# Reordering TensorE's work behind a gather, packing a transposed operand from four chunks into three, and two idle matmuls in the last tile

## The chip, the cores and the metric

The kernel runs on one core of a Trainium2 chip. The metric is the device time of one execution in microseconds (us). Lower is better. The engines are named as in the profile: PE is TensorE's matmul side, PEld its weight loads, DVE is VectorE, ACT is ScalarE, POOL is GpSimd, SP is SyncE.

## What is computed

A recommendation model's top part: 27 embedding rows of 128 numbers are looked up for each of 512 samples, all pairwise dot products within a sample are taken, 16 dense numbers are appended, and three layers follow.

```python
e = jnp.stack([tbl_0[ids[:, 0]], ..., tbl_26[ids[:, 26]]], axis=1)   # (512, 27, 128), fp32
dot_products = jnp.einsum('bnd,bmd->bnm', e, e)
r, c = np.tril_indices(27, k=-1)
z = dot_products[:, c, r]                                           # (512, 351)
h = jnp.concatenate([z, dense_ctx], axis=1)                         # (512, 367)
h = jnp.maximum(h @ W_top1 + b_top1, 0.0)                           # (512, 512)
h = jnp.maximum(h @ W_top2 + b_top2, 0.0)                           # (512, 256)
y = h @ W_top3                                                      # (512, 1)
```

## The kernel before

The 512 samples are four tiles of 128 (`T = 4`). Every engine has its own hand-written list of calls, and semaphores join the lists. Nothing is reordered by a planner: the order of the calls in the source is the order on the engine.

**The one-hot part.** Nine small tables (1000 rows) are looked up by matmul: DVE and ACT make one-hot matrices, PE multiplies (`one_hot`, L456 and L460), ACT copies the result into `embT` (L224). The other 18 tables are gathered on POOL by one indirect DMA for each table and tile, 72 in all (L214), in tile order. Gathered rows are turned on PE in groups of up to four (`transposes(t, g)`, L470; five groups a tile, the last of two) and copied into `embT` by ACT or DVE (L228). Tile 0's groups and three of tile 1's are worked in between the one-hot matmuls.

**Behind it**, for each tile t:

- `products(t, u)`, u = 0 and 1: 64 small matmuls of 32 x 27 each, one sample each (L487). They are in fp32, and PE runs each as two passes, so the profile counts 128 matmuls and 128 weight loads for a call. ACT copies the result to `prod` (L351), DVE merges the other half of the products over it (L252).
- `turn(t)`: DVE turns 32 x 32 blocks from `prod` to `pairs` in one instruction (L261, 14 columns of 32), then PE transposes `pairs` in four chunks of 112 (L501), and ACT and DVE copy two chunks each to `pairsT` (L356, L266). The 14 columns hold 448 rows, of which 351 are products that the first layer needs and the rest are gaps with zero weights.
- `layer1(t, ms)` (L511): four output blocks of 128, each over the `KC = 4` chunks. `layer2(t)` (L523): 2 output blocks over 4 chunks. `layer3(t)` (L532): one output row over 2 chunks. In between ACT and DVE add the bias and apply ReLU (L365, L275, L373, L283); DVE copies the result row to `y_sb` (L288).

The Gram results use four PSUM banks (`GB = 4`). The transposes of gathered rows use two banks behind the one-hot part, the layers two others, and layer 3's row stands in a corner of one of the latter, which is why `turn(t)` waits for `y_ready` of the tile before. At its start PE runs `WARM = 11` matmuls of 512 columns whose results nobody reads (L538).

Waits that a matmul cannot carry itself are instructions of their own on PE (`pe.wait_ge` twice before one matmul). A fp32 matmul is four PE instructions (two passes, each a load and a matmul), a transpose or a one-hot matmul two.

Of the kernel before, what the change touches and what calls it, by code (L numbers as in the profile page):

```python
# [16 lines left out]
UNIT = 16  # L17
GB = 4
UNITS = GROUPS // UNIT
# [4 lines left out]
MERGED = HALF + 1  # L24
KC = 4
KR = MERGED * SLOT // KC
assert KR * KC == MERGED * SLOT and KR + ND <= P

# [17 lines left out]
MC2 = H2 // P  # L46
WARM = 11


# [16 lines left out]
def tower(nc, ids, ids_t, dense_t, tbls, w1, w2, cols, pick, y):  # L66
# [21 lines left out]
    with ExitStack() as ctx:  # L88
# [22 lines left out]

        pairs = sb("pairs", [P, 2, MERGED * SLOT])

# [15 lines left out]
        layer = [fill[:, 2 + i, :] for i in range(2)]  # L129
        sums3 = layer[1][0:1, 2 * P:3 * P]  # L130

# [22 lines left out]
        prod_a = sem("prod_a")  # L154
        merged = sem("merged")
        pairs_ready = sem("pairs_ready")
        turned = sem("turned")
# [15 lines left out]
        @block.sync  # L173
        def _(sp):
            def load_onehot(n):
                f = ONEHOT[n]
                if n >= NT:

                    sp.wait_ge(filled, FILL_NO[("oh", n - NT)] + 1)
                sp.dma_start(ids_bc[:, n % NT, :], ids_t[f:f + 1, :].broadcast_to([P, B])).then_inc(idsbc_in[n], 16)  # L180
                rows = tbls[f].rearrange("(p c) d -> p (c d)", c=CH)
                sp.dma_start(table[0:CA, n % NT, :], rows[0:CA]).then_inc(table_in[n], 16)
                sp.dma_start(table[CA:CR, n % NT, :], rows[CA:CR]).then_inc(table_in[n], 16)

# [7 lines left out]
            sp.dma_start(pairsT[KR:KR + ND, :, 0, :], dense_t.rearrange("n (t b) -> n t b", t=T)).then_inc(w_in, 16)  # L192
# [39 lines left out]
        def _(dve):  # L232
# [23 lines left out]
            def turn(t):  # L256
                dve.wait_ge(merged, UNITS * (t + 1))
                if t >= 2:

                    dve.wait_ge(turned, t - 1)  # L260
                nc.vector.transpose(pairs[:, t % 2, :].rearrange("p (c i) -> p c i", i=SLOT),  # L261
                                    prod[:, t % 2, :, :].rearrange("p g c -> p c g")).then_inc(pairs_ready, 1)

            def take_turned(t):
                dve.wait_ge(turned, t + 1)
                nc.vector.tensor_copy(pairsT[0:KR, t, 2:4, :],  # L266
                                      layer[1][0:KR, 0:2 * P].rearrange("p (k b) -> p k b", k=2)).then_inc(pairsT_v, 1)

# [34 lines left out]
            take_turned(0)  # L303
            take_products(1, 0)
            take_layer1(0)
            take_transposes((2, 0))
            take_layer2(0)
            take_products(1, 1)
            turn(1)
            take_layer3(0)  # L310
            take_transposes((2, 1))
            take_turned(1)
            take_transposes((2, 2))
            take_layer1(1)
            take_transposes((2, 3))
            take_layer2(1)
            take_transposes((2, 4))
            take_layer3(1)
            take_products(2, 0)
            take_transposes((3, 0))  # L320
            take_products(2, 1)
            turn(2)
            take_transposes((3, 1))
            take_turned(2)
            take_transposes((3, 2))
            take_layer1(2)
            take_layer2(2)
            take_layer3(2)
            take_transposes((3, 3), (3, 4))
            for u in range(UNITS):  # L330
# [8 lines left out]
        def _(act):  # L339
# [14 lines left out]
            def take_turned(t):  # L354
                act.wait_ge(turned, t + 1)
                nc.scalar.copy(pairsT[0:KR, t, 0:2, :],  # L356
                               layer[0][0:KR, 0:2 * P].rearrange("p (k b) -> p k b", k=2)).then_inc(pairsT_a, 1)

# [46 lines left out]
            act.wait_ge(zeros_ready, 1)  # L405
            take_products(0, 0)
            take_transposes((1, 3))
            take_products(0, 1)
            take_transposes((1, 4))
            take_turned(0)  # L410
            take_products(1, 0)
            take_layer1(0)
            take_transposes((2, 0))
            take_layer2(0)
            take_products(1, 1)
            take_transposes((2, 1))
            take_turned(1)
            take_transposes((2, 2))
            take_layer1(1)
            take_transposes((2, 3))  # L420
            take_layer2(1)
            take_transposes((2, 4))
            take_products(2, 0)
            take_transposes((3, 0))
            take_products(2, 1)
            take_transposes((3, 1))
            take_turned(2)
            take_transposes((3, 2))
            take_layer1(2)
            take_layer2(2)  # L430
            take_transposes((3, 3), (3, 4))
            for u in range(UNITS):
# [6 lines left out]
        def _(pe):  # L439
# [51 lines left out]
            def turn(t):  # L491
                pe.wait_ge(pairs_ready, t + 1)
                if t == 0:

                    pe.wait_ge(taken_a, len(EARLY))
                else:

                    pe.wait_ge(h2_a, t)
                    pe.wait_ge(y_ready, t)
                for k in range(KC):  # L500
                    last = nc.tensor.transpose(layer[k // 2][0:KR, k % 2 * P:(k % 2 + 1) * P],  # L501
                                               pairs[:, t % 2, k * KR:(k + 1) * KR], ident[:])
                last.then_inc(turned, 1)

            def layer1(t, ms):
                pe.wait_ge(pairsT_a, t + 1)
                pe.wait_ge(pairsT_v, t + 1)
                for m in ms:
                    for k in range(KC):
                        rows = KR + ND if k == 0 else KR  # L510
# [16 lines left out]
            def layer3(t):  # L527

                pe.wait_ge(h2_v, t + 1)
                pe.wait_ge(h2_a, t + 1)  # L530
                for m2 in range(MC2):
# [5 lines left out]
            for _ in range(WARM):  # L537
                nc.tensor.matmul(fill[:, 3, :].rearrange("p (r c) -> p r c", r=4), ident[:],  # L538
                                 ident[:].unsqueeze(1).broadcast_to([P, 4, P]), start=True, stop=True)
            for what in EARLY:  # L540
# [4 lines left out]
            pe.wait_ge(zeros_ready, 1)  # L545
            products(0, 0)
            transposes(1, 3)
            products(0, 1)
# [10 lines left out]
            transposes(2, 1)  # L559
            turn(1)  # L560
            transposes(2, 2)
            layer1(1, (0, 1))
            layer1(1, (2, 3))
            transposes(2, 3)
            layer2(1)
            transposes(2, 4)
            layer3(1)
            products(2, 0)
            transposes(3, 0)
            products(2, 1)  # L570
            transposes(3, 1)
            turn(2)
            transposes(3, 2)
            layer1(2, (0, 1))
            layer1(2, (2, 3))
            layer2(2)
            layer3(2)
            transposes(3, 3)
# [50 lines left out]
```

## Time and profile before

| | |
|---|---|
| median of 3 runs | 178.98 us (178.2 to 181.49) |
| the profiled execution | 177.67 us |
| its span, first to last instruction | 175.8 us |
| outside the span | 1.87 us |
| mean granted TensorE clock | 0.806 of full |
| busy: PE, PEld, DVE, ACT, POOL | 104.6, 82.8, 55.5, 48.3, 78.8 us |

All durations below are of the one profiled execution. The span has three stages: the one-hot part (0 to 52 us), a stretch in which POOL goes on gathering and PE is mostly idle (52 to 110 us), and the rest of tiles 0 to 3 on PE (110 to 176 us). "Issue" as the cause of an idle time means that the engine waited for nothing that the profile shows.

### The profile page before, as it was taken

Reading aid. Unit: us, or ns where it says so; the run is one execution under the profiler, and the core shown is the slowest. Engines: PE = TensorE matmul, PEld = TensorE weight load, DVE = VectorE, ACT = ScalarE, POOL = GpSimd, SP = SyncE. Lnnn points to the kernel's source line nnn. Section 1 sums busy time; section 2 is a strip of 40 time slices with the busy share of each in tenths; the row PEclk is TensorE's granted clock in tenths of the full one; section 3 lists DMA queues with packets and bytes.
Section 4 is the critical chain, followed back from the end, with each engine's and each line's share of the span. In section 5 each row is a group of like instructions: output and inputs, shape, how many; then the busy total and the mean of one; then the engine's idle time right before and its main releaser. Section 6 shows DMA issues by size and latency. Waiting matters only on the chain.

```text
span 175.8 us, 3411 instructions
## 1 busy us (share of the span) xinstructions
PE 104.6 (59%) x1486; PEld 82.8 (47%) x1486; DVE 55.5 (32%) x112; ACT 48.3 (27%) x84; POOL 78.8 (45%) x79
## 2 busy tenths in 40 slices
PE   6999999599982111100000002958969547972794
PEld 2448887487862110000000001748869437951693
DVE  5586978989700000000000000150343134123111
ACT  0581985999931000000000000311322111220010
POOL 4778877878777777777777730000000000000000
PEclk9999999999999555555555555599999996999579
DMA  4999999995121212121212110000000000000000
GB/s 76 278 256 267 346 273 247 240 241 122 34 60 49 60 45 60 45 60 45 60 45 60 51 38 0 4 4 4 4 0 0 4 4 4 0 4 4 0 4 0
DMA packets 6571, 13.59 MB, mean 77 GB/s; under 512 B 2422, under 2 KB 2998, under 8 KB 6428
## 3 DMA queue, kind: packets, MB, share of 16 engines
q1 hardware_dynamic: 4252, 8.64, 19.4%
q0 software_dynamic: 2304, 4.72, 9.9%
q8 instruction: 12, 0.20, 0.4%
q14 instruction: 3, 0.02, 0.0%
HBM read 13.36 MB, written 0.00 MB: 76 GB/s over the span
## 4 chain that ended last, share of the span: by engine, by line
issue 39%; PE 31%; POOL 21%; DVE 4%; DMA 3%; ACT 1%
POOL emb L214 21%; PE fill L511 10%; PE gram L487 10%; PE fill L523 4%; PE fill L470 3%; PE fill L501 2%; DVE pairs L261 2%; DMA emb<-tbl_dram,ids_sb 1%; DMA ids_sb<-ids_dram 1%; PE fill L532 1%; DVE prod L252 1%; DVE h L283 1%; ACT prod L351 1%; DVE pairsT L266 0%; ACT embT L228 0%
## 5 line engine op out<-in xcount | busy, mean ns | idle before, releaser
L214 POOL DMA_INDIRECT emb<-tbl_dram,ids_sb x72 | 78.0, 1084 | 23.2 <-issue 21.6
L487 PE MATMUL gram<-embT 128*32 128x27 f32 x1024 | 18.5, 202 | 56.0 <-issue 55.5
L487 PEld LDWEIGHTS gram<-embT 128*32 128x32 f32 x1024 | 14.9, 117 | 60.1 <-issue 59.1
L252 DVE COPY_PREDICATED prod<-pick_sb,gram 128x224 f32<-128x224 int32 x8 | 3.3, 407 | 79.7 <-ACT prod L351 79.7
L238 DVE TENSOR_SCALAR onehot<-ids_bc,row_no 125x512 fp32r<-125x512 int32 x63 | 26.0, 482 | 6.2 <-DMA ids_bc<-ids_t_dram 3.9
L351 ACT COPY prod<-gram 128x224 f32<-128x224 f32 x8 | 2.8, 345 | 72.6 <-PE gram L487 72.6
L511 PE MATMUL fill<-pairsT,w_sb 112*128 112x128 f32 (+1 forms) x128 | 18.3, 309 | 2.4 <-issue 1.6
L456 PE MATMUL fill<-onehot,high 125*128 125x512 f32 x72 | 19.2, 408 | 0.0
L511 PEld LDWEIGHTS fill<-pairsT,w_sb 112*128 112x128 f32 (+1 forms) x128 | 17.5, 222 | 3.3 <-issue 1.8
L460 PE MATMUL fill<-onehot,low 125*128 125x512 f32 x72 | 17.9, 390 | 0.0
L460 PEld LDWEIGHTS fill<-onehot,low 125*128 125x128 f32 x72 | 13.5, 188 | 2.9
L456 PEld LDWEIGHTS fill<-onehot,high 125*128 125x128 f32 x72 | 13.0, 188 | 3.2 <-issue 0.5
L470 PE MATMUL fill<-ident,emb 128*128 128x128 f32 x72 | 12.6, 299 | 2.5 <-DMA emb<-tbl_dram,ids_sb 2.4
L538 PE MATMUL fill<-ident 128*128 128x512 f32 x22 | 11.6, 692 | 1.6 <-POOL ident L204 1.6
L224 ACT COPY embT<-fill 128x512 f32<-128x512 f32 x9 | 10.0, 1112 | 7.8 <-PE fill L460 7.5
L241 DVE TENSOR_TENSOR low<-table,high 125x1024 fp32r<-125x1024 f32 x9 | 10.9, 1216 | 1.3 <-ACT high L391 1.3
L470 PEld LDWEIGHTS fill<-ident,emb 128*128 128x128 f32 x72 | 9.0, 151 | 4.9 <-issue 4.1
L391 ACT CAST high<-table 125x512 fp32r<-125x512 f32 x18 | 10.4, 628 | 2.7 <-DMA table<-tbl_dram 2.5
L228 ACT COPY embT<-fill 128x512 f32<-128x512 f32 (+1 forms) x14 | 9.4, 670 | 5.6 <-PE fill L470 5.5
L538 PEld LDWEIGHTS fill<-ident 128*128 128x128 f32 x22 | 4.9, 228 | 7.5 <-issue 5.9
L523 PE MATMUL fill<-h,w_sb 128*128 128x128 f32 x64 | 8.4, 279 | 0.0
L275 DVE TENSOR_SCALAR h<-fill,cols_sb 128x128 f32<-128x128 f32 x8 | 2.4, 347 | 18.5 <-PE fill L511 18.5
(25 smaller groups left out, 51.1 us busy)
## 6 DMA issues: line engine op xcount, KB each, us to landing
table<-tbl_dram SPq DMA_DIRECT2D x9, 448.0 KB
ids_bc<-ids_t_dram SPq DMA_DIRECT2D x9, 256.0 KB, 5.0
emb<-tbl_dram,ids_sb POOLq DMA_INDIRECT x72
w_sb<-w_dram SPq DMA_DIRECT2D x1, 1024.0 KB
w_sb<-w_dram SPq DMA_DIRECT2D x1, 512.0 KB
table<-tbl_dram SPq DMA_DIRECT2D x9, 52.0 KB
ids_sb<-ids_dram SPq DMA_DIRECT2D x1, 54.0 KB, 2.1
pairsT<-dense_t_dram SPq DMA_DIRECT2D x1, 32.0 KB
```

The costliest lines, as they stand in the source:

```text
L214: nc.gpsimd.indirect_dma_start(out=emb[:, t % EB, n, :], out_offset=None, in_=tbls[f], in_offset=bass.IndirectOffsetOnAxis(ap=ids_sb[:, t, ...
L224: copy(embT[:, :, :, what[1]].rearrange("p t b -> p (t b)"), fill[:, bank(i), :]).then_inc(taken, 1)
L238: nc.vector.tensor_scalar(onehot[:, n % 2, c, :], ids_bc[0:CR, n % NT, :], row_no[0:CR, c:c + 1], None, ALU.is_equal).then_inc(onehot_v, 1)
L241: nc.vector.tensor_tensor(low[:, n % 2, :], table[:, n % NT, :], high[:, n % 2, :].bitcast(fp32), ALU.subtract).then_inc(low_ready, 1)
L391: nc.scalar.copy(high[:, n % 2, a:a + half], table[:, n % NT, a:a + half]).then_inc(high_ready, 1)
L456: nc.tensor.matmul(fill[:, bank(i), :], high[:, n % 2, c * D:(c + 1) * D], onehot[:, n % 2, c, :], start=(c == 0), stop=False)
L460: last = nc.tensor.matmul(fill[:, bank(i), :], low[:, n % 2, c * D:(c + 1) * D], onehot[:, n % 2, c, :], start=False, stop=(c == CH - 1))
L470: last = nc.tensor.transpose(fill[:, bank(i), (n - a) * P:(n - a + 1) * P], emb[:, t % EB, n, :], ident[:])
L487: last = nc.tensor.matmul(gram[i % GB][SLOT * s:SLOT * (s + 1), g, :], embT[:, t, b, :], embT[:, t, b, 0:F], start=True, stop=True)
L511: last = nc.tensor.matmul(layer[m // 2][:, m % 2 * P:(m % 2 + 1) * P], w1_sb[0:rows, k, m * P:(m + 1) * P], pairsT[0:rows, t, k, :], start ...
L523: last = nc.tensor.matmul(layer[m2][:, 0:P], w2_sb[:, m, m2 * P:(m2 + 1) * P], h1[:, m, :], start=(m == 0), stop=(m == MC - 1))
L538: nc.tensor.matmul(fill[:, 3, :].rearrange("p (r c) -> p r c", r=4), ident[:], ident[:].unsqueeze(1).broadcast_to([P, 4, P]), start=True, ...
```

## The change

Four things are changed.

1. **Three chunks.** `prod`'s 13 full columns are turned so that the rows follow each other without gaps (row 13*i + c), and the half column is laid behind them by a second DVE instruction, which waits for the first. 364 rows and the 16 dense ones fit three chunks (128, 128, 108), so `turn` has three PE transposes, `layer1` twelve matmuls rather than sixteen for a tile, DVE copies one chunk rather than two, and `w1` is 768 KB rather than 1024 KB. The host lays the weights out to match.
2. **The order.** On PE both halves of `products` stand together for every tile. In tile 0 they run ahead of the last transposes of tile 1; in tile 1 both halves run ahead of layer 1 of tile 0; `turn(1)` moves ahead of layer 3 of tile 0; further transposes of the next tile are spread between the layers. DVE's and ACT's lists are changed to match.
3. **PSUM.** Layer 3's row gets a bank of its own, `GB` goes from 4 to 3. `turn(t)` waits for `h2_v` of the tile before in place of `y_ready`, and `layer3` waits for `y_ready`.
4. **Idle matmuls.** Two matmuls of 512 columns whose result is not read (`TURN_BUSY = 2`, four passes) stand between `products(3, 1)` and `turn(3)`.

```diff
-GB = 4
+GB = 3
-KC = 4
-KR = MERGED * SLOT // KC
+TURNED = HALF * SLOT
+ROWS = HALF * F + HALF
+KC = 3
+KL = ROWS - (KC - 1) * P
+TURN_BUSY = 2
...
-        sums3 = layer[1][0:1, 2 * P:3 * P]
+        sums3 = pb("sums3", [1, P])[:]
...
-                nc.vector.transpose(pairs[:, t % 2, :].rearrange("p (c i) -> p c i", i=SLOT),
-                                    prod[:, t % 2, :, :].rearrange("p g c -> p c g")).then_inc(pairs_ready, 1)
+                by_column = prod[:, t % 2, :, :].rearrange("p g c -> p c g")
+                nc.vector.transpose(pairs[:, t % 2, :].rearrange("p (i c) -> p c i", c=HALF),
+                                    by_column[:, 0:HALF, :]).then_inc(columns_ready, 1)
+                dve.wait_ge(columns_ready, t + 1)
+                nc.vector.transpose(pairs[:, t % 2, HALF * F:HALF * F + SLOT],
+                                    by_column[:, HALF, :]).then_inc(pairs_ready, 1)
...
                     pe.wait_ge(h2_a, t)
-                    pe.wait_ge(y_ready, t)
+                    pe.wait_ge(h2_v, t)
                 for k in range(KC):
-                    last = nc.tensor.transpose(layer[k // 2][0:KR, k % 2 * P:(k % 2 + 1) * P],
-                                               pairs[:, t % 2, k * KR:(k + 1) * KR], ident[:])
+                    rows = KL if k == KC - 1 else P
+                    last = nc.tensor.transpose(layer[k // 2][0:rows, k % 2 * P:(k % 2 + 1) * P],
+                                               pairs[:, t % 2, k * P:k * P + rows], ident[:])
...
+            def keep_busy(b, count):
+                for _ in range(count):
+                    nc.tensor.matmul(fill[:, b, :].rearrange("p (r c) -> p r c", r=4), ident[:],
+                                     ident[:].unsqueeze(1).broadcast_to([P, 4, P]), start=True, stop=True)
...
-            products(1, 0)
+            for u in range(UNITS):
+                products(1, u)
             layer1(0, (0, 1))
             layer1(0, (2, 3))
             transposes(2, 0)
             layer2(0)
-            products(1, 1)
+            turn(1)
...
                 products(3, u)
+            keep_busy(0, TURN_BUSY)
             turn(3)
```

The order on PE, from the last one-hot matmul to tile 2's products. `gram0` to `gram3` are the products' banks, `fill<-ident,emb` are transposes of gathered rows, `fill<-ident,pairs` those of `turn`, and the last three kinds are layers 1, 2 and 3. The kernel before:

```order
L487 MATMUL gram0<-embT 32x27 x64
L470 MATMUL fill<-ident,emb 128x128 x4
L487 MATMUL gram1<-embT 32x27 x64
L470 MATMUL fill<-ident,emb 128x128 x2
L501 MATMUL fill<-ident,pairs 112x128 x4
L487 MATMUL gram2<-embT 32x27 x64
L511 MATMUL fill<-pairsT,w1_sb 128x128 x16
L470 MATMUL fill<-ident,emb 128x128 x4
L523 MATMUL fill<-h1,w2_sb 128x128 x8
L487 MATMUL gram3<-embT 32x27 x64
L532 MATMUL fill<-h2,cols_sb 1x128 x2
L470 MATMUL fill<-ident,emb 128x128 x4
```

The changed kernel, the same stretch on PE:

```order
L494 MATMUL gram0<-embT 32x27 x64
L494 MATMUL gram1<-embT 32x27 x64
L477 MATMUL fill<-ident,emb 128x128 x6
L509 MATMUL fill<-ident,pairs 128x128 x2
L509 MATMUL fill<-ident,pairs 108x128
L494 MATMUL gram2<-embT 32x27 x64
L494 MATMUL gram0<-embT 32x27 x64
L519 MATMUL fill<-pairsT,w1_sb 128x128 x12
L477 MATMUL fill<-ident,emb 128x128 x4
L531 MATMUL fill<-h1,w2_sb 128x128 x8
L509 MATMUL fill<-ident,pairs 128x128 x2
L509 MATMUL fill<-ident,pairs 108x128
```

Tile 1's second half of products moved from behind layer 2 of tile 0 to ahead of its layer 1, the turn of tile 1 now directly follows layer 2 of tile 0, and layer 1 has 12 matmuls.

The order on PE for the end of tile 2 and all of tile 3, the kernel before:

```order
L487 MATMUL gram<-embT 32x27 x64
L470 MATMUL fill<-ident,emb 128x128 x4
L487 MATMUL gram<-embT 32x27 x64
L470 MATMUL fill<-ident,emb 128x128 x4
L501 MATMUL fill<-ident,pairs 112x128 x4
L470 MATMUL fill<-ident,emb 128x128 x4
L511 MATMUL fill<-pairsT,w_sb 128x128 x16
L523 MATMUL fill<-h,w_sb 128x128 x8
L532 MATMUL fill<-h,cols_sb 1x128 x2
L470 MATMUL fill<-ident,emb 128x128 x6
L487 MATMUL gram<-embT 32x27 x128
L501 MATMUL fill<-ident,pairs 112x128 x4
```

The changed kernel, the same stretch:

```order
L494 MATMUL gram<-embT 32x27 x128
L477 MATMUL fill<-ident,emb 128x128 x8
L509 MATMUL fill<-ident,pairs 128x128 x2
L509 MATMUL fill<-ident,pairs 108x128
L477 MATMUL fill<-ident,emb 128x128 x4
L519 MATMUL fill<-pairsT,w_sb 128x128 x12
L477 MATMUL fill<-ident,emb 128x128 x4
L531 MATMUL fill<-h,w_sb 128x128 x8
L543 MATMUL sums<-h,cols_sb 1x128 x2
L477 MATMUL fill<-ident,emb 128x128 x2
L494 MATMUL gram<-embT 32x27 x128
L549 MATMUL fill<-ident 128x512 x2
```

The transposes between the two halves of tile 2's products moved behind both, four of the next ones moved between layers 1 and 2, and the two idle matmuls stand behind tile 3's products.

## Rows read from the trace of the kernel before

**Rows 1.** Three stages: us, busy us of each engine (instructions), granted clock, DMA share, GB/s

```profile
0.00:52.00 52.00, 48.00 (x192) 34.23 (x192) 38.27 (x74) 34.86 (x53) 40.19 (x39) 1.00 0.80 205
52.00:110.00 58.00, 8.20 (x100) 5.54 (x104) 0.00 (x0) 1.27 (x2) 38.62 (x41) 0.54 0.17 48
110.00:176.00 66.00, 48.38 (x1202) 43.02 (x1201) 17.22 (x38) 12.15 (x30) 0.00 (x0) 0.89 0.01 3
```

**Rows 2.** Timeline, end of the slow stretch: start, us, instruction, count, idle before

```profile
101.87 0.94 POOL L214 DMA_INDIRECT emb<-tbl_dram,ids_sb  x1 [0.30 <-issue]
...
103.58 0.20 PE L487 MATMUL gram<-embT 128*32 128x27 f32 x1 [2.60 <-issue]
...
109.88 0.79 PE L487 MATMUL gram<-embT 128*32 128x27 f32 x40 [1.15 <-issue]
```

**Rows 3.** The chain that ended last, 110 to 162 us: start, us, what

```profile
110.66 1.05 PE fill L470 x4
111.71 1.86 PE gram L487 x128
...
116.12 1.22 PE gram L487 x82
...
117.75 1.60 issue
...
128.61 0.63 PE fill L501 x4
...
129.84 3.81 PE fill L511 x32
133.65 0.44 PE fill L470 x4
134.09 1.80 PE fill L523 x16
...
137.99 1.97 issue
...
141.95 1.84 issue
...
158.23 1.93 issue
```

**Rows 4.** PE's timeline between two stops, 139 to 144 us

```profile
139.96 0.25 PE L487 MATMUL gram<-embT 128*32 128x27 f32 x3 [1.97 <-issue]
140.14 0.66 PE L470 MATMUL fill<-ident,emb 128*128 128x128 f32 x4
140.72 1.22 PE L487 MATMUL gram<-embT 128*32 128x27 f32 x120
```

**Rows 5.** DMA queue that carries instructions: packets, MB, share of 16 engines' span

```profile
q8 instruction: 12, 0.20, 0.4%
```

**Rows 6.** The chain that ended last, tiles 2 and 3

```profile
145.92 1.10 PE fill L501 x4
...
161.11 0.35 ACT prod L351
...
161.93 0.95 DVE pairs L261
...
162.93 1.11 PE fill L501 x4
164.06 0.43 DVE pairsT L266
...
164.63 6.05 PE fill L511 x32
...
173.21 0.61 PE fill L532 x4
```

**Rows 7.** A stretch at the lower clock: columns as in rows 1

```profile
162.50:169.30 6.80, 5.76 (x26) 5.38 (x27) 0.80 (x2) 1.00 (x3) 0.00 (x0) 0.50 0.01 2
```

**Rows 8.** The first idle matmuls (L538) alone: PE, PEld, clock, DMA share, GB/s

```profile
5.50:9.00 3.50, 3.50 (x9) 1.56 (x9) 1.00 1.03 266
```

More of the change, by code:

```diff
@@ L24 @@
 MERGED = HALF + 1
-KC = 4
-KR = MERGED * SLOT // KC
-assert KR * KC == MERGED * SLOT and KR + ND <= P
+TURNED = HALF * SLOT
+ROWS = HALF * F + HALF
+KC = 3
+KL = ROWS - (KC - 1) * P
+assert 0 < KL and KL + ND <= P
 ROWS_OH = 1000
@@ L110, in tower @@
         prod = sb("prod", [P, 2, GROUPS, MERGED])
-        pairs = sb("pairs", [P, 2, MERGED * SLOT])
+        pairs = sb("pairs", [P, 2, TURNED])
         pairsT = sb("pairsT", [P, T, KC, P])
@@ L307, in _ @@
             take_layer2(0)
-            take_products(1, 1)
-            turn(1)
+            take_turned(1)
+            take_transposes((2, 1))
             take_layer3(0)
-            take_transposes((2, 1))
-            take_turned(1)
+            take_layer1(1)
             take_transposes((2, 2))
-            take_layer1(1)
+            take_layer2(1)
             take_transposes((2, 3))
-            take_layer2(1)
+            take_layer3(1)
             take_transposes((2, 4))
[L318 to L321, printed above, removed]
+            for u in range(UNITS):
+                take_products(2, u)
             turn(2)
-            take_transposes((3, 1))
+            take_transposes((3, 0), (3, 1))
             take_turned(2)
@@ L355, in take_turned @@
                 act.wait_ge(turned, t + 1)
-                nc.scalar.copy(pairsT[0:KR, t, 0:2, :],
-                               layer[0][0:KR, 0:2 * P].rearrange("p (k b) -> p k b", k=2)).then_inc(pairsT_a, 1)
+                nc.scalar.copy(pairsT[:, t, 0:2, :],
+                               layer[0][:, 0:2 * P].rearrange("p (k b) -> p k b", k=2)).then_inc(pairsT_a, 1)
             def take_layer1(t):
@@ L405, in _ @@
             act.wait_ge(zeros_ready, 1)
[L406 to L409, printed above, removed]
+            for u in range(UNITS):
+                take_products(0, u)
+            take_transposes((1, 3), (1, 4))
             take_turned(0)
-            take_products(1, 0)
+            for u in range(UNITS):
+                take_products(1, u)
             take_layer1(0)
@@ L414, in _ @@
             take_layer2(0)
-            take_products(1, 1)
+            take_turned(1)
             take_transposes((2, 1))
-            take_turned(1)
+            take_layer1(1)
             take_transposes((2, 2))
-            take_layer1(1)
-            take_transposes((2, 3))
             take_layer2(1)
[L422 to L426, printed above, removed]
+            take_transposes((2, 3), (2, 4))
+            for u in range(UNITS):
+                take_products(2, u)
+            take_transposes((3, 0), (3, 1))
             take_turned(2)
@@ L530, in layer3 @@
                 pe.wait_ge(h2_a, t + 1)
+                if t > 0:
+                    pe.wait_ge(y_ready, t)
                 for m2 in range(MC2):
@@ L534, in layer3 @@
                 last.then_inc(layer3_ready, 1)
+            def keep_busy(b, count):
+                for _ in range(count):
+                    nc.tensor.matmul(fill[:, b, :].rearrange("p (r c) -> p r c", r=4), ident[:],
+                                     ident[:].unsqueeze(1).broadcast_to([P, 4, P]), start=True, stop=True)
             pe.wait_ge(ident_ready, 1)
-            for _ in range(WARM):
-                nc.tensor.matmul(fill[:, 3, :].rearrange("p (r c) -> p r c", r=4), ident[:],
-                                 ident[:].unsqueeze(1).broadcast_to([P, 4, P]), start=True, stop=True)
+            keep_busy(3, WARM)
             for what in EARLY:
@@ L545, in _ @@
             pe.wait_ge(zeros_ready, 1)
-            products(0, 0)
+            for u in range(UNITS):
+                products(0, u)
             transposes(1, 3)
-            products(0, 1)
             transposes(1, 4)
@@ L551, in _ @@
             turn(0)
-            products(1, 0)
+            for u in range(UNITS):
+                products(1, u)
             layer1(0, (0, 1))
@@ L556, in _ @@
             layer2(0)
-            products(1, 1)
+            turn(1)
+            transposes(2, 1)
             layer3(0)
-            transposes(2, 1)
-            turn(1)
-            transposes(2, 2)
             layer1(1, (0, 1))
             layer1(1, (2, 3))
+            transposes(2, 2)
+            layer2(1)
             transposes(2, 3)
-            layer2(1)
+            layer3(1)
             transposes(2, 4)
-            layer3(1)
-            products(2, 0)
+            for u in range(UNITS):
+                products(2, u)
             transposes(3, 0)
-            products(2, 1)
             transposes(3, 1)
@@ L575, in _ @@
             layer1(2, (2, 3))
+            transposes(3, 3)
             layer2(2)
             layer3(2)
-            transposes(3, 3)
             transposes(3, 4)
@@ L608 @@
             hi, lo = max(ORDER[i], ORDER[j]), min(ORDER[i], ORDER[j])
-            row = SLOT * c + i
-            w1[row % KR, row // KR] = w_top1[hi * (hi - 1) // 2 + lo]
+            w1[HALF * F + i if c == HALF else HALF * i + c] = w_top1[hi * (hi - 1) // 2 + lo]
             pick[:, i, c] = j >= HALF
-    w1[KR:KR + ND, 0] = w_top1[F * (F - 1) // 2:]
+    w1[ROWS:ROWS + ND] = w_top1[F * (F - 1) // 2:]
+    w1 = w1.reshape(KC, P, H1).transpose(1, 0, 2)
     ids = give("ids_dram", inputs["ids"])
```

18 lines of the change are left out of this document (10 added, 8 removed).

## The prediction, made before the changed kernel was run

> **What bounds the kernel now.** I read three views in this order: the busy time by stage, the chain that ended last, and PE's timeline where that chain says "issue".
>
> By stage [rows 1], the first 52 us are the one-hot part, in which PE is busy 48.0 us. The change leaves it alone but for a weight load 256 KB smaller. From 52 to 110 us PE is busy 8.2 of 58 us, DVE 0, and POOL gathers. From 110 to 176 us POOL is done, and PE is busy 48.4 of 66 us. All that the change touches is in this third stage, and only what stands on its chain counts.
>
> The second stage is strange. PE stands in `products(0, 0)`, which waits for nothing, yet its matmuls come 2.80 us apart (idle 2.60) until shortly after POOL's last gather at 101.87 [rows 2]. At 109.88 it suddenly runs 40 in 0.79 us. I can't name the cause. But PE's program up to the end of `products(0, 0)` is the same in both kernels, instruction for instruction, and so are the gathers. I take that stretch as unchanged, and count from 110.66, where the first of tile 1's transposes starts [rows 3].
>
> In the third stage the chain is nearly all PE, with four idle pieces put down to "issue": 1.60, 1.97, 1.84 and 1.93 us, 7.34 in all [rows 3]. Between the one that ends at 139.96 and the next, which begins at 141.95, PE ran 3 + 4 + 120 = 127 passes [rows 4]. Each is a load and a matmul, so 254 instructions, and two separate waits make 256. The queue that carries instructions moved 12 packets, 0.20 MB [rows 5], which is 16 KB each. So PE's program comes in **blocks of 256 instructions**, and these four pieces are PE waiting for a block. From the start of `products(1, 0)` at 116.12, four instructions ahead of a block's end, to the end of the stop at 117.75 + 1.60 = 119.35 it is 3.24 us. From 139.96 to 141.95 + 1.84 = 143.79 it is 3.83. I read this as a new block being there 3.2 to 3.8 us after the one before it is entered. Work with long passes covers that: 32 passes of layer 1 take 3.81 us [rows 3]. Products don't: 128 passes, a whole block, take some 1.3 us (1.22 for 120 [rows 4]), which leaves about 2 us idle.
>
> The Trainium skill, "Runtime: NRT & Kernel Launch", section "Instruction fetch mechanics", also has 16 KiB blocks of 256 instructions, but says that the cost of crossing from one to the next is "mostly hidden". Here it isn't. By that rule the later stops of the walk below would vanish and the result would be about 8 us lower.
>
> **The change part by part**, as a walk from 110.66. The places of the blocks' ends in the new program follow from counting on from the stops of before.
>
> *Tile 0.* The second half of the products follows at once: 110.66 + 1.86 at the lower clock [rows 3] = 112.5. From the end of products to the start of the turn on PE it is 162.93 - 161.11 = 1.82 us (ACT copy, DVE merge, DVE transpose) [rows 6]. The DVE transpose is now two instructions with a wait between them. No row shows the short one, or an output written with a stride of 13. Less than nothing is excluded, since the elements are almost the same and an instruction is added. At the other end I set a second full transpose, 0.95 us [rows 6]. I take 0.2, near the low end, as 416 + 32 columns are the 448 of before. So `turn(0)` is at 114.6. The six transposes of tile 1 fit ahead of it (110.66 to 111.71 for four at the lower clock). Three chunks take 0.47 in place of 0.63, and `products(1, 0)` starts at 115.1 in place of 116.12: **1.0 us won**.
>
> *Tile 1's products in one piece.* They cross two block ends, one 7 instructions in, one 6 instructions into layer 1. First stop: ends at 115.1 + 3.24 = 118.35. Second: 1.24 us of products, then layer 1 stops until 118.35 + 3.2 to 3.8, and I take 122.0. Before, layer 1 ran on from 119.35. So this place **loses 2.6 us**, a new stop of some 2.3 us, though the second half of the products, 1.3 us, is now behind us.
>
> *Layers of tile 0.* Layer 1 has 24 passes rather than 32. At 3.81/32 = 0.119 each [rows 3] that is 2.86 us, **0.95 less for each tile**. Then transposes 0.44 and layer 2 1.80: end at 126.85. The bias step (about ACT's 0.35, and 0.1 of signalling) is now open, since the products that covered it are gone: `turn(1)` at 127.3. Before it was 128.61, because ACT, DVE merge and transpose stood behind the second half of the products. **1.3 us ahead.**
>
> *Tile 1.* Turn 0.47, transposes 0.44, layer 3 about 0.5 (0.61 [rows 6] at most), and layer 1 starts at 128.7 (before 129.84). The copies to `pairsT` are under the transposes. Then 2.86 + 0.44 + 1.80 = 133.8 (before 135.89). Behind it transposes 0.44, layer 3 0.5, two transposes 0.3 and their copy some 0.5: tile 2's products start at 135.7. **1.0 us ahead** of 136.7 (137.99 less 125 passes).
>
> *Tile 2's products in one piece.* Block ends fall 30 instructions into either half. The first stop ends 3.3 after the start, as before (136.7 to 139.96): 139.0. The other 113 passes end at 140.15. The next block end is now behind them, in `transposes(3, 2)`, and due only at 142.8. Before, a second stop of 1.84 stood ahead of the products' end at 144.1. Turn at 140.15 + 1.82 + 0.2 = 142.2, with eight transposes of 0.88 beneath, against 145.92 [rows 6]: **3.7 ahead**. Layer 1 at 143.3, layer 1, transposes, layer 2: 148.5. Layer 3, two transposes and copies some 1.9: products of tile 3 at 150.4. Before it was 156.5 (158.23 less 173 passes). **6.1 ahead.**
>
> *Tile 3.* The block end falls 401 instructions into the products. Stop until 150.4 + 3.75 = 154.15 (before 156.5 to 160.16, 3.7), the last passes 0.6: end at 154.8, **6.3 ahead**. ACT's and DVE's chain of 1.82 + 0.2 makes the turn due at 156.8. Beneath it are the four passes of 512 columns. Nine took 3.50 us at full clock [rows 8], 0.39 each, so 1.6 us, and they end at 156.4: hidden by 0.4 us. Then the clock: before, it fell at 162.5 behind the stop of 1.93 and the idle wait for the turn, and stayed at 0.50 until 169.3 [rows 7]. The last turn took 1.10 in place of 0.63, layer 1 6.05 in place of 3.81 [rows 3, 6]. If the idle matmuls keep it up, the turn takes 0.47, the copies 0.43 and some 0.15, and layer 1 starts at 157.85 (164.63 before, 6.8 ahead), takes 2.86 and not 6.05: **10.0 ahead**. The rest is as before.
>
> *Nothing:* `GB = 3`, since by then each bank was merged long ago, hidden by the stops above (without them a wait of some 0.4). `layer3`'s wait for `y_ready`: DVE copies the row long ahead. DVE and ACT get their calls in the order in which PE delivers; at 17.2 and 12.2 us busy of 66 [rows 1] they queue for at most one copy. The smaller `w1` is covered by the gathers.
>
> **Sum.** 1.0 - 2.6 + 2.9 (to `turn(1)`) - 0.3 (to tile 2's products) + 2.7 (tile 2's stop and turn) + 2.4 (its layers) + 0.2 + 0.5 (to the last layer 1) + 3.2 (that layer 1) = 10.0. The span becomes 165.8, the profiled execution 177.67 - 10.0 = 167.7. The median of the runs is 1.3 above that execution, so the forecast is 178.98 - 10.0 = **169.0**.
>
> **Rivals.**
>
> *The clock falls all the same.* Two stops of 2 us in tile 1 lie nearer to each other than those before which the clock fell at 162.5, and in tile 3 the four passes leave the stop itself idle. In tile 3: 24 passes at 6.05/32 = 0.189 rather than 0.119 cost 1.7, the turn 0.35, and the idle matmuls at half speed take 3.2, 1.2 past the turn's due time: 3.2, so **172.2**. In tile 1 as well, 1.7 more: 173.9. Against it: the stop of 1.60 at 117.75 left the clock up, and the idle matmuls fill most of the second gap.
>
> *Stops at their longer price, and a dear transpose.* Three stops 0.6 longer, and 0.75 more for the DVE transpose at three tiles where it is open: 4.0, so **173.0**.
>
> *The slow stretch lasts longer (the slower side).* If the stretch ends by a place in the program or by what the queue behind holds, not by the gathers' end, then the 64 products that now follow directly may be caught in it. One pass costs 2.80 there [rows 2]. The new order wins back 10.0, so from four more slow passes on the change loses; ten give 178.98 - 10 + 28 = **197**. For it: nobody knows why the stretch ends. Against it: the program is identical until then, and 40 of `products(0, 0)`'s own passes already ran fast.
>
> *The order does nothing.* If the chain's gains in tiles 1 and 2 are eaten by waits that I don't see (`turn(1)` and `layer3` have new ones) and the clock falls, the shorter layer 1 is left: 3.8 less, so **175.2 to 177**.
>
> **How the numbers follow.** Forecast 0.55 (167 to 171.5), clock 0.2, longer stops 0.1, order does nothing 0.08, slow stretch 0.05, and 0.02 for a result far below. The range is 166.5 (all stops at 3.2) to 174.5 (clock falling in both places). No change within 2% (175.4 to 182.6) is about what a measurement of this kernel can't tell from none. Faster 0.86, same 0.08, slower 0.06.
>
> **What would show it.** Right: an idle piece of some 2 us inside tile 1's products and another at the head of layer 1, one inside tile 2's and one inside tile 3's, and the granted clock at 1.00 through the last layer 1, with its 24 passes near 2.9 us. Wrong: a slow stretch that ends later than 110 us, DVE transposes well over 1.1 us together, the idle matmuls ending behind `pairs`, or a last layer 1 of 4.5 us.

## The result, and the profile after

The changed kernel takes 172.63 us (median of 4 runs, 171.64 to 174.67), the kernel before beside it 179.5 (178.2 to 181.49). The ratio is 0.962, with a 95% interval of 0.950 to 0.974: **faster**. The profiled execution took 171.64 us, its span is 169.8. The forecast was 169.0, the range 166.5 to 174.5. Medians in this document are over all runs of a kernel, ratios and their intervals over its fast runs alone (those within 1.5% of its fastest).

The three stages of the profile after, in the columns of [rows 1] (the cuts are where its stages end), and two short stretches of tile 3:

```profile
0.00:52.00 52.00, 48.47 (x192) 34.45 (x192) 38.16 (x74) 34.66 (x53) 40.68 (x37) 1.00 0.78 199
52.00:111.40 59.40, 8.44 (x89) 5.61 (x89) 0.00 (x0) 1.52 (x2) 39.71 (x42) 0.52 0.16 48
111.40:169.80 58.40, 43.12 (x1173) 36.69 (x1173) 17.62 (x42) 12.18 (x30) 0.00 (x0) 0.93 0.01 3
156.90:160.30 3.40, 3.40 (x59) 1.99 (x59) 1.56 (x3) 0.35 (x1) 0.00 (x0) 0.50 0.02 5
161.80:164.80 3.00, 3.00 (x27) 3.00 (x28) 0.03 (x1) 0.63 (x2) 0.00 (x0) 1.00 0.00 0
```

The third stage is 58.4 us long. Before, it was 175.8 - 109.88 = 65.9. So it gave 7.5 us, and the stage ahead of it took 1.55 back: the slow stretch, in which PE's passes come up to 2.80 us apart, ended at 111.43 and not at 109.88. POOL's last gather began 1.5 later too, at 103.40 and not at 101.87 [rows 2]. The last two lines show the clock low during the idle matmuls and full in the last layer 1.

The chain that ended last, after (start, us, what), where [rows 3, 6] show it before:

```profile
116.66 1.32 PE gram L494 x85
117.98 2.45 issue
120.43 1.26 PE gram L494 x81
121.69 0.53 PE fill L519 x3
122.22 1.78 issue
124.00 2.61 PE fill L519 x21
...
129.37 0.52 PE fill L509 x3
...
137.87 1.39 PE gram L494 x87
139.26 1.93 issue
...
152.62 1.90 PE gram L494 x117
154.52 2.35 issue
156.87 0.96 PE gram L494 x41
157.84 3.16 PE fill L549 x4
161.00 0.34 PE fill L509 x3
...
161.80 2.93 PE fill L519 x24
```

There are two stops in tile 1, one of them three passes into layer 1, one in tile 2, one in tile 3. Then come the idle matmuls (L549): four passes in 3.16 us. Layer 1 takes 2.93 where [rows 6] has 6.05.

### The profile page after: what moved, and what is told of

It is laid out like the page before. It is cut to its first block, busy times and chain, and to the rows that moved or that the text cites. A ratio compares the mean times of both kernels' runs of the same rounds, so it can differ in the third digit from the quotient of the medians.

```text
span 169.8 us, 3351 instructions
## 1 busy us (share of the span) xinstructions
PE 100.0 (59%) x1454; PEld 76.8 (45%) x1454; DVE 55.8 (33%) x116; ACT 48.4 (28%) x84; POOL 80.4 (47%) x79
## 4 chain that ended last, share of the span: by engine, by line
issue 41%; PE 29%; POOL 23%; DMA 3%; DVE 2%; ACT 0%
POOL emb L219 23%; PE gram L494 11%; PE fill L519 7%; PE fill L531 4%; PE fill L477 3%; PE fill L549 2%; DMA emb<-tbl_dram,ids_sb 1%; PE sums L543 1%; DMA ids_sb<-ids_dram 1%; PE fill L509 1%; DVE h L292 1%; DVE pairs L267 1%; DVE embT L233 0%; DVE prod L257 0%; ACT pairsT L365 0%
## 5 line engine op out<-in xcount | busy, mean ns | idle before, releaser
L219 POOL DMA_INDIRECT emb<-tbl_dram,ids_sb x72 | 79.6, 1106 | 23.1 <-issue 21.6
L549 PE MATMUL fill<-ident 128*128 128x512 f32 x26 | 15.4, 757 | 1.6 <-POOL ident L209 1.6
L477 PE MATMUL fill<-ident,emb 128*128 128x128 f32 x72 | 11.8, 290 | 3.5 <-DMA emb<-tbl_dram,ids_sb 3.5
L519 PE MATMUL fill<-pairsT,w_sb 128*128 128x128 f32 (+1 forms) x96 | 11.9, 279 | 2.3 <-issue 1.8
L519 PEld LDWEIGHTS fill<-pairsT,w_sb 128*128 128x128 f32 (+1 forms) x96 | 11.1, 191 | 2.9 <-issue 2.2
L549 PEld LDWEIGHTS fill<-ident 128*128 128x128 f32 x26 | 6.2, 248 | 9.1 <-issue 7.4
L531 PEld LDWEIGHTS fill<-h,w_sb 128*128 128x128 f32 x64 | 7.6, 192 | 0.2 <-DVE h L284 0.2
```

The lines of the kernel that those rows point to most:

```text
L219: nc.gpsimd.indirect_dma_start(out=emb[:, t % EB, n, :], out_offset=None, in_=tbls[f], in_offset=bass.IndirectOffsetOnAxis(ap=ids_sb[:, t, ...
L477: last = nc.tensor.transpose(fill[:, bank(i), (n - a) * P:(n - a + 1) * P], emb[:, t % EB, n, :], ident[:])
L531: last = nc.tensor.matmul(layer[m2][:, 0:P], w2_sb[:, m, m2 * P:(m2 + 1) * P], h1[:, m, :], start=(m == 0), stop=(m == MC - 1))
L549: nc.tensor.matmul(fill[:, b, :].rearrange("p (r c) -> p r c", r=4), ident[:], ident[:].unsqueeze(1).broadcast_to([P, 4, P]), start=True, ...
```

## The experiments

Single runs of one kernel spread by 2 to 8.5 us here. The profiles show one source: the slow stretch ends with POOL's gathers, whose last one began anywhere from 101.9 to 106.8 us. I therefore also give the **tail**, the time from PE's return to its full pace (the first of a long row of passes without gaps) to the end of the span: 65.9 us before, 58.4 after. A tail still holds what the granted clock did. It was at 0.50 when the pace came back and rose only later, at 115.9 us in the changed kernel's profile.

### The parts of the change, one at a time

These four ran beside each other on one chip, and the slow stretch was there in all of them. First the changed kernel again.

> The changed kernel once more, as the yardstick for the three beside it. Expected 172.6 us (0.96 of before), with four stops of 1.8 to 2.5 us behind the start of tile 1's products.

Measured: 173.03 us median, ratio 0.949 (0.938 to 0.961). Tail 171.8 - 112.97 = 58.8. There are four stops, but not of the expected length:

```profile
118.58 1.95 PE gram L494 x131
120.53 1.21 issue
121.73 1.92 PE gram L494 x125
...
124.59 0.99 issue
...
140.85 2.20 issue
...
156.39 2.35 issue
```

The granted clock was 0.50 until 124.9 us here, and tile 1's products took 1.9 us for a block rather than 1.3. The two stops shrank from 2.45 and 1.78 to 1.21 and 0.99. From the start of the products to the end of the first stop it is 3.15 us, from there to the end of the second 3.85, at the lower clock as at the full one (3.77 and 3.57). So PE waits for something that comes at its own pace, and a stop is what the passes leave of it. That is also why the tail is only 0.4 us longer, though the clock was low for 7.4 us more of it (11.9 rather than 4.5 us).

Without the idle matmuls:

```diff
-TURN_BUSY = 2
+TURN_BUSY = 0
```

> The changed kernel without the two idle matmuls ahead of the last turn. Theory: in the profiled execution they ran at the lower clock, took 3.2 us and ended 1.0 us past the turn's due time, but the clock was back up for layer 1. Without them the turn comes 1.0 earlier and the clock stays low through it and layer 1, as before the change: 24 passes at 0.189 rather than 0.122 us cost 1.6, the turn 0.4. Net 1.0 us slower, 173.6. Rival (the clock comes back by itself, the matmuls only delay): 1.0 us faster, 171.6. Second rival (they were what brought most of the gain): 176 or more.

Measured: ratio 0.956 (0.940 to 0.971). Its six runs lie between 171.6 and 178.4 us, the median of all is 177.37. Tail 175.7 - 113.34 = 62.4. The end of its chain, and the clock there:

```profile
160.63 1.00 PE gram L494 x41
...
163.71 0.92 PE fill L509 x3
...
165.09 5.48 PE fill L519 x24
```

```profile
160.30:170.60 10.30, 7.38 (x85) 6.86 (x85) 1.84 (x4) 1.34 (x4) 0.00 (x0) 0.50 0.01 2
122.80:129.60 6.80, 5.29 (x58) 4.94 (x46) 1.55 (x3) 0.97 (x3) 0.00 (x0) 0.50 0.02 5
```

From the end of the products (161.6) the turn comes after 2.1 us rather than 3.1, and then layer 1 takes 5.48 rather than 2.93 and the turn 0.92 rather than 0.5. Net 2.0 us in tile 3, as by the first theory and twice its price. The other 1.6 of the tail goes with the clock falling at 122.8, ahead of anything that the idle matmuls could touch: layer 1 of tile 0, behind its stop, took 4.46 us and not 2.61. The runs alone don't settle the price. The median is 4.3 us above that of `again`, which would be the second rival (176 or more), but two of the six runs (171.6 and 173.6) are as fast as the changed kernel's, and the intervals of the ratios overlap. The profiles show the 2.0 for tile 3, in one execution of each. What the idle matmuls do to the clock is firmer: the last layer 1 took 2.93 us in all ten profiles that have them and three chunks, and 5.48 and 5.03 in the two that have three chunks and no idle matmuls (here and in the next kernel).

The three chunks alone:

```diff
-TURN_BUSY = 2
+TURN_BUSY = 0
...
-            keep_busy(0, TURN_BUSY)
...
(PE's, DVE's and ACT's calls behind the one-hot part in the order of before)
```

> The three chunks alone, with the calls in the order of before, three banks for the products and layer 3's row in a bank of its own, no idle matmuls. Theory: 8 of 32 passes of layer 1 go for each tile: 0.95 in tiles 0 and 1, about 1.1 in tile 2, 1.5 in tile 3 at the lower clock, the turn 0.2 shorter each time, the second DVE transpose 0.24 longer on the chain of three tiles: 4.5 us less than before, so 175.0 us (ratio 0.975). Rival (the packing is hidden under the stops for instruction blocks): less than 2 us less, 177.5 or more.

Measured: 174.73 us median, ratio 0.968 (0.960 to 0.975). Tail 173.8 - 114.90 = **58.9**, that is 7.0 less than before and only 0.1 to 0.5 more than the whole change. By the medians the whole change is 1.7 us ahead of it. The two profiled executions also differ by 1.9 in where the slow stretch ended, so the runs can't tell how much of the 1.7 is of the kernel. Its idle pieces put down to "issue", behind 115 us:

```profile
119.27 1.55 issue
124.18 0.58 issue
142.10 1.37 issue
157.14 2.35 issue
```

The first lies ahead of tile 0's turn, as does 1.31 before, and ends as DVE's transposes of `pairs` end (120.72), so it isn't counted as a stop. The other three make 4.3 us, where [rows 3] has 7.34. The sixteen passes that shorter layers take out of two tiles moved the block ends, and tile 2 has one stop in place of two. That is 3.0 us. Layer 1 gives the rest: 5.03 for 6.05 in the last tile, 2.9 for 4.15 and 3.81 in tiles 2 and 1, about 0.8 in tile 0, 4.0 in all. A part of that is the clock, which fell once more in the profile before (145.4 to 148.9).

The new order alone, with the idle matmuls, on four chunks:

```diff
-KC = 3
...
+KC = 4
+KR = MERGED * SLOT // KC
...
(one DVE transpose, 448 rows with gaps, two chunks for DVE to copy, as before)
```

> The new order with the idle matmuls, three banks and layer 3's own bank, but four chunks with gaps as before. Theory: the changed kernel plus 8 passes of layer 1 in each of four tiles (0.12 each, 3.8 us in all) plus 0.5 for the turns, less 0.7 for the second DVE transpose: 172.6 + 3.6 = 176.2 us (ratio 0.98). Rival (the order is worth nothing, the packing all): the time of before, 179.5. Rival (the order is all): 173.

Measured: 180.33 us median beside 181.97, ratio 0.998 (0.987 to 1.009). Tail 177.9 - 114.15 = 63.8, 2.1 less than before. Its stops:

```profile
120.60 2.11 issue
124.39 1.89 issue
...
143.40 2.37 issue
147.52 1.98 issue
...
163.06 1.94 issue
```

That is 10.3 us of stops, 3 more than before, with two in each of tiles 1 and 2. What the idle matmuls win (layer 1 of tile 3 takes 3.81 us here, 6.05 before) the extra stops take back, and 2.1 us of the tail is left. The runs show no gain that is clear of noise. I had expected 176.2: the sum of parts failed, because the block ends fall elsewhere when the program is longer.

### What the slow stretch hangs on

Six profiles so far put PE's return to its full pace 7.9 to 8.15 us behind the start of the last gather. Three kernels were to tell why.

```diff
             pe.wait_ge(zeros_ready, 1)
+            a, e = TG[NTG - 1]
+            pe.wait_ge(gathered[T - 1][NTG - 1], 16 * (e - a))
             for u in range(UNITS):
                 products(0, u)
```

> The changed kernel, with one more wait on PE: it starts the products of tile 0 only when the last gathered rows of tile 3 have landed. So far the slow stretch ended 7.9 to 8.1 us after the start of POOL's last gather, in six profiled executions in which that gather started anywhere from 101.9 to 106.8 us. Theory 1 (PE's instructions come slowly only while gathers are under way, and a landing is some 3 us after the start): PE starts 3 us after the last gather's start, runs both halves of the products in 3.7 us at the lower clock and one stop for a block of 2 us: 2 to 4 us faster than the changed kernel, 169 us. Theory 2 (PE has a fixed number of slow instructions to get through, some 100 at 0.7 us or more each, whenever it comes to them): 50 us or more slower, 225 us. Theory 3 (the slow state ends 8 us after the last gather, whatever PE does): no change, 172 us.

The same with tile 2's last rows, `gathered[T - 2]`:

> The same wait, but for the last gathered rows of tile 2, some 25 us earlier (PE starts the products near 83 us). Theory 1 expects the first 30 to 40 passes fast, then a slow stretch from 83 us until 8 us after the last gather, and no change in time, 172. Theory 2 expects the slow stretch to last 55 us from 83 on, 197. A third possibility is that no slow stretch appears at all: then products of tile 0 end at 86 us, and the time falls to some 165.

And without the gathers of tile 3:

```diff
-            for t in range(T):
+            for t in range(T - 1):
...
-                pe.wait_ge(gathered[t][g], 16 * (e - a))
+                pe.wait_ge(gathered[t % EB][g], 16 * (e - a))
```

> The changed kernel without tile 3's 18 gathers (54 rather than 72); tile 3 is computed on tile 0's gathered rows, so its results are not the reference's. Theory 1: the slow stretch ends 18 x 1.25 = 22.5 us earlier, near 89 us, and the whole takes some 150 us. Theory 2 (a fixed number of slow instructions): the slow stretch still ends near 110 us, 172 us.

They landed on another chip, and there the **kernel before itself takes 131.78 us** (12 runs, 130.6 to 134.9), 48 less. Measured: `hold` 171.8 (six runs), `hold_mid` 148.1 and `no_tile3` 123.4 (one run each). No slow stretch is seen in any of the three profiles. Here is `hold` on that chip, PE's timeline:

```profile
108.76 2.13 PE L494 MATMUL gram<-embT 128*32 128x27 f32 x142 [51.71 <-issue]
112.75 1.80 PE L494 MATMUL gram<-embT 128*32 128x27 f32 x114 [1.86 <-issue]
```

So the three say nothing of what the stretch hangs on. They showed that it isn't a property of the kernel alone. `hold` was therefore run again and came to a third chip, where the kernel before takes 182.56 us.

> The changed kernel with PE held until the last gathered rows of tile 3 have landed. On a chip without the slow stretch it takes 171.8, some 43 us more than the kernel that isn't held. On a chip with the slow stretch it tells what the stretch hangs on. Theory 1 (PE is slow only while gathers are under way): PE starts full speed at the last gather's start + 3 us: 2 to 4 us less than the changed kernel. Theory 2 (a fixed number of slow instructions): 50 us or more added. Theory 3 (PE's slow state lasts until 8 us after the last gather whatever it does): no change.

Measured: 174.9 us, beside 172.0 for the changed kernel. PE's timeline:

```profile
108.55 0.75 PE L494 MATMUL gram<-embT 128*32 128x27 f32 x40 [51.65 <-issue]
109.96 0.20 PE L494 MATMUL gram<-embT 128*32 128x27 f32 x1 [0.65 <-issue]
...
113.46 0.20 PE L494 MATMUL gram<-embT 128*32 128x27 f32 x1 [0.50 <-issue]
114.16 3.10 PE L494 MATMUL gram<-embT 128*32 128x27 f32 x212 [0.50 <-issue]
```

The gathers had landed, PE ran 40 passes, and then it was slow all the same, until 114.16. The last gather began at 105.95, 8.2 us ahead. Theory 1 falls, since no gather was under way, and so does theory 2, since far fewer than 100 instructions were slow. Theory 3 stands: the state ends some 8 us behind the start of the last gather, whether PE is held or not. Holding PE back wins nothing.

This profile also answers a question of the forecast. Its clock fell at 124.8, in tile 1, and stayed at 1.00 through tile 3. There the idle matmuls ran as foretold:

```profile
163.34 1.98 PE L549 MATMUL fill<-ident 128*128 128x512 f32 x4
165.51 0.55 PE L509 MATMUL fill<-ident,pairs 128*128 128x128 f32 x3 [0.20 <-DVE pairs L271]
```

At the full clock the four passes take 1.98 us and end 0.2 ahead of `pairs`, in `hold_mid` and `shift` too. At the lower one they take 3.1 to 3.5 and end behind it.

### Is the new order worth anything?

```diff
 (the three chunks alone, as above, and)
+            keep_busy(0, TURN_BUSY)
             turn(3)
```

> The three chunks and the idle matmuls, but the calls in the order of before. It separates the new order from the rest. From the profiles, from the end of the slow stretch to the end of the span it is 65.9 us before, 58.4 and 58.8 changed, 58.9 with the three chunks alone. Theory: the idle matmuls win 2.0 here as in the comparison of the changed kernel with and without them, so 57 us and a ratio to before near 0.945 to 0.955, as good as the changed kernel or 1.5 us better, and the new order is worth nothing. Rival: the order is worth 2 to 3 us, and this kernel stays 2 us behind the changed one.

On the chip without the slow stretch: 127.96 us, ratio 0.958 (0.950 to 0.967). The stages there, columns as in [rows 1]:

```profile
0.00:52.00 52.00, 47.90 (x188) 34.04 (x189) 38.11 (x74) 34.64 (x52) 40.71 (x37) 1.00 0.82 197
52.00:110.00 58.00, 41.07 (x1072) 35.63 (x1072) 13.90 (x33) 11.73 (x26) 40.34 (x43) 0.85 0.21 52
```

PE is busy 41 of the 58 us in which it is busy 8.2 in [rows 1], and what it waits for most is the gathered rows:

```profile
PE fill L479 <- DMA emb<-tbl_dram,ids_sb: 14.3, 8, 4.0
```

Then, beside the changed kernel on the third chip:

> The changed kernel again, beside the two below on whatever chip they get. The last four kernels ran on another chip than those ahead of them, and there the kernel before takes 131.8 us and no slow stretch is seen in the kernels that don't hold PE back. If this chip has the slow stretch: 173 us, ratio 0.955. If not: PE is free from 56 us on and waits for gathered rows instead. Then both halves of tile 1's products wait for nothing that comes late (tile 1 has landed by 64 us), tile 2's wait for its last rows, landed near 83 us, and tile 3's for the last, landed near 108; only tile 3's own work stands behind those: transposes, products with a stop, the turn, its layers. There the change saves 8 passes of layer 1 and keeps the clock: 3 to 5 us less than 131.8, so 128, ratio 0.97.

> The three chunks and the idle matmuls in the order of before, beside the changed kernel. On a chip without the slow stretch it took 128.0 (ratio 0.958). With the slow stretch: 171 to 172 if the new order is worth nothing, and 174 or more if the order is worth 2 us or more.

Measured: 171.96 and 172.96 us, the first at a ratio of 0.947 (0.936 to 0.957), tails 58.7 and 59.9. The second's layer 1 of tile 0 ran at the lower clock in the profiled execution (4.13 us for 21 passes, 2.61 in the first), which is more than the whole difference. By the medians the new order, with the three chunks and the idle matmuls in place, is worth 1 us at most. By the fastest runs (169.94 and 169.57) it is worth nothing.

### Do the stops follow the blocks?

```diff
+SHIFT = 14
...
             keep_busy(3, WARM)
+            for _ in range(SHIFT):
+                nc.tensor.matmul(fill[0:1, 3, 0:1], ident[:, 0:1], ident[:, 0:1], start=True, stop=True)
```

> The changed kernel with 14 matmuls of one column behind the first idle ones, results not read: 56 more instructions on PE ahead of everything else, which moves every block's end 56 instructions earlier in the program, and costs well under 1 us itself. Theory of the blocks: the next block is asked for some 50 instructions behind a block's start. In the changed kernel that point stood 43 instructions inside tile 1's products, now it stands ahead of them, so the block behind is there in time: tile 1's products and the head of layer 1 show one stop of 2 us rather than two with 3.8 to 4.5 together; tiles 2 and 3 keep one stop each, tile 3's some 0.3 longer. From the end of the slow stretch to the end of the span 56.8 us rather than 58.7: 171 us on a chip that has the slow stretch. And the slow stretch itself: so far some 40 passes ran fast ahead of it, which is where the point 50 instructions behind a block's start lies (the products start 30 behind that start). If the slow state hangs on that point, only 10 to 14 passes run fast now. If it hangs on a count from the products' start, it stays 40. Rival to both: the stops come from the products' own length, wherever the blocks end; then two stops remain in tile 1, the tail stays at 58.7, and the time is that of the changed kernel.

This one came to a fourth chip, again without the slow stretch (before 132.11 us), so nothing is learned of the stretch. Measured: 126.06 us, ratio 0.963 (0.946 to 0.981). PE's timeline:

```profile
68.11 1.61 PE L495 MATMUL gram<-embT 128*32 128x27 f32 x103
71.50 2.09 PE L495 MATMUL gram<-embT 128*32 128x27 f32 x128 [1.78 <-issue]
75.23 0.54 PE L495 MATMUL gram<-embT 128*32 128x27 f32 x25 [1.64 <-issue]
75.70 4.48 PE L520 MATMUL fill<-pairsT,w_sb 128*128 128x128 f32 x24
...
110.87 1.67 PE L495 MATMUL gram<-embT 128*32 128x27 f32 x172 [0.56 <-issue]
114.62 0.91 PE L495 MATMUL gram<-embT 128*32 128x27 f32 x84 [2.08 <-issue]
```

Tile 1's stop moved from pass 131 to pass 103, tile 3's from 200 to 172: 28 passes, 56 instructions, to the pass. Between two stops there are 128 passes. So the rival falls, and the stops do hang on the blocks of 256. But my count of stops was wrong. Tile 1 still has two (1.78 and 1.64, 3.4 in all, where the changed kernel has 4.2 in its first profile). In tile 2 the second block end slipped back into the products (stops of 2.48 and 1.50 us). For tile 1 my guess is that the point at which the next block is asked for stands on the wait that heads the products, not ahead of it; no run tests that. The order, a shift and a packing each only move these places.

## Why the prediction was right, and by its own steps

**Span and blocks.** The reading that "PE's program comes in blocks of 256 instructions" held to the pass, in the changed kernel as in the shifted one. That the stops are waits for a block has a second sign in the trace before: around the stop that begins at 137.99, one packet of 16 KB went over the instruction queue (stretch 137.0 to 139.9):

```profile
q8 instruction: 1, 0.02, 2.1%
```

Behind 110 us that queue moved ten packets in the kernel before, and there were four stops. The other six left no stop. The changed kernel's four stops stood at the places of the walk. Together they were 8.5 us (2.45, 1.78, 1.93, 2.35); by the walk, some 8.

**Step by step.** The walk's times against the profile: `products(1, 0)` 115.1 and 116.6, layer 1 of tile 0 resumed 122.0 and 124.0, `turn(1)` 127.3 and 129.4, tile 2's products 135.7 and 137.9, `turn(2)` 142.2 and 144.5, tile 3's products 150.4 and 152.6, the last layer 1 157.85 and 161.8, end 165.8 and 169.8. So it is 4.0 late, of which 1.55 is the start. The forecast gain of 10.0 us came to 6.0 in the profiled spans and 6.9 in the medians.

**"I take that stretch as unchanged."** Right for the program, too bold for the time. The stretch ends with POOL's last gather, which moves by 5 us between executions; here it was 1.5 later. That is not of the change.

**"Hidden by 0.4 us"** was the term that failed. The idle matmuls ran at the lower clock, which fell at 156.9 behind the stop of 2.35, and took 3.16 rather than 1.6: 1.0 us lost. Even at the full clock four passes take 1.98 (`hold_b`), so the margin was 0.2. This is half of the rival "the clock falls all the same". The other half did not come: at 160.3 it was full again, and layer 1 took 2.93 (2.86 foretold).

**Stops.** The first in tile 1 ended 0.6 later than foretold, the one in tile 3 0.5, with 0.3 for the passes behind it: small steps towards the rival of longer stops. The two DVE transposes took 0.93 + 0.23 against 0.95 and added 0.2 to the chain, as taken.

**"The order does nothing"** was priced at 175.2 to 177 and given 0.08, for the time. The time is not there, but the claim about the order is nearly true. I gave tile 2's single stop (2.7 us) to the order. The three chunks alone get it too, because they shorten the program. So the total was right and its shares were wrong, and that the total held is in part luck: packing 7.0 of the tail, idle matmuls 1.1 to 2.0 in tile 3 where layer 1 would else run slowly, order at most 1. (The 1.1 is the same stretch, from the end of the products to the end of layer 1, in `pack_only` and `pack_idle_b`: 8.5 and 7.35 us.) The three don't add up to the whole, since each moves the block ends for the others.

**The rule of the Trainium skill** ("Runtime: NRT & Kernel Launch", "Instruction fetch mechanics") that a crossing is "mostly hidden" does not hold for these rows of 128x27 matmuls. All profiled kernels show stops there, most of 1.1 to 2.7 us, the shortest 0.5. Six of the ten blocks behind 110 us in the kernel before do cross without a stop. Its block size agrees.

**Left open:** what the slow stretch is. It was there in the first comparison and on two chips since, in every kernel profiled, and on two other chips in none (the kernel before was not profiled there, only timed). Each chip was used in one comparison only, so nothing here tells the chip from the moment. It costs some 50 us of 180. Its end follows the last gather's start by 7.9 to 8.4 us in nine profiles, held or not. That PE should wait on something left by POOL's gathers is argued from this, not shown. Another sign points at the supply of instructions: in all nine profiles a packet on the instruction queue starts within 0.7 us of the end of the first quick passes, at 53.8 and 53.2 us before, at 109.6 and 109.3 in `hold_b`. So the slow stretch may set in where the next block is asked for. `shift` was to test that and came to a chip without the stretch. It wasn't tried to fill the stretch with other work or to spread the gathers over time. Whether the whole change gains as much on a chip without the stretch wasn't measured either: only two relatives of it ran there, at 0.958 and 0.963.

## What to carry to other kernels

Short matmuls in a long row outrun the supply of instructions: here 128 passes take 1.3 us, and the next 256 instructions were there 3.1 to 4.1 us after a block was entered. Count instructions on PE as a cost of their own, and prefer an edit that removes them to one that reorders them; before crediting a new order with a stop that went, count where the blocks' ends fall. And when one execution differs from the next, look for the stage: a tail measured from a common event tells 1 to 2 us apart where the runs spread by 8, if the falls of the clock within it are looked up first.

## What the hardware showed that I had not expected

The same kernel took 131.8 and 132.1 us on two chips and 179.5 to 182.6 on the others. The difference is about as long as the stretch in which PE issues a pass, at first every 0.7 to 2.8 us and from 90 us on every 2.80, with nothing to wait for. It sets in after some 40 passes, even when PE starts only after all the gathers have landed.

The granted clock does not fall in the same place in every execution. Kernels alike up to there had the same stop of 2.35 us inside tile 3's products. Behind it the clock fell at 156.9 in the changed kernel, and it stayed at 1.00 in `hold_b`. In tile 1 it was the other way round: it fell at 124.8 in `hold_b` and at 122.8 in `no_idle`, and stayed at 1.00 in the changed kernel behind a stop of 2.45. The longest idle piece ahead of any of these three falls was 2.45 us.
